# Softmax attention on one core: the maxima's negation one reduction later, sums normalised a pair at a time, maxima sixteen ahead in place of twenty

## The chip, the cores and the metric

The kernel runs on one core of one Trainium2 chip. The metric is device time in microseconds of one execution; the median of three executions of the kernel before is 1983.7 us (1981.62 to 1983.73).

## The reference, cut to what matters

Two blocks run one after the other; the change lies in the second block's attention (16 heads of 8 features each). Every query of every head takes a softmax over 2048 keys:

```
q = _apply_rope(_rms_norm(x @ wq.T), cos, sin) / sqrt(8)
k = _apply_rope(_rms_norm(x @ wk.T), cos, sin)
scores = einsum('bqhd,bkhd->bhqk', q, k)
attn = softmax(scores, axis=-1)
out = einsum('bhqk,bkhd->bqhd', attn, v) @ wo.T
```

Two sequences of 2048 tokens with 16 heads give 32 square score matrices of 2048 x 2048, which the kernel computes twice: once to find each query's maximum, once, transposed and with the maximum subtracted, for the exponential.

## The kernel before, in words

`softmax_attention` (from line 1322) works on pairs of heads: 16 pairs (8 of each sequence), each cut into 4 chunks of 512 queries, 64 chunks in all. In what follows n is a chunk whose exponentials are under way, m one whose maxima are.

**Maxima.** A chunk has 32 units. For unit a TensorE multiplies 128 queries with 512 keys (`maximum`, line 1489) into one of four banks (3 to 6), and VectorE reduces the bank to one column (line 1631). TensorE's unit u waits until the reduction of unit u - 4 is done (line 1486). Behind the 32nd reduction VectorE waits for all of them (line 1635) and takes the largest over the key blocks, negated (`at_neg`, line 1636). GpSimd turns that into three bfloat16 parts (`parts`, lines 1421 to 1431: five small operations, each waiting for the one ahead). TensorE transposes the parts (`shifts`, line 1499), and ScalarE copies them in two operations into spare rows of the queries (`take_shifts`, line 1582). So every score comes out with the maximum already subtracted.

**Scores.** A chunk has 32 steps s. TensorE makes 128 keys x 512 queries (`score`, line 1509) into one of three banks (0 to 2), ScalarE takes the exponential (line 1590), and every second step TensorE multiplies with the values (`weigh`, line 1525, eight matmuls at a time). A bank is used again when the turn three turns back has been read (`free_bank`). The transposed parts and the transposed sums take turns in the same three banks.

**Sums.** ScalarE copies the chunk's result out of bank 7 (`take_sums`, line 1596) after exponential 3 of the next chunk, TensorE transposes it (line 1536) after step 11, ScalarE copies that to rows (`read_sums`, line 1602). VectorE takes the reciprocal of the 8 sums (`invert`, line 1624), and GpSimd multiplies the 64 columns with them (`normalise_sums`, line 1439). VectorE's `invert(m - 2)` stands right behind the negation of chunk m.

**Order on TensorE.** It is written out by hand. A prologue issues all 32 maxima of chunk 0 and the first AHEAD = 20 of chunk 1, `shifts(0)` behind the maximum 10 and scores 0 to 3 beside the last four. The main loop then issues one score and one maximum at each step: beside score s of chunk n stands maximum s - 4 + AHEAD counted from chunk n + 1's first. With AHEAD = 20 the last maximum of chunk n + 1 (number 31) stands at s = 15, the first one of chunk n + 2 (number 0) at s = 16. `shifts(n + 1)` stands behind step 27, where with AHEAD = 20 the maximum number 11 of chunk n + 2 stands.

GpSimd's order in chunk n is: `parts(n + 1)`, `normalise_sums(n - 1)`, at the first chunk of a pair two copies of the next pair's values (line 1411), and in the last two pairs four gathers of rows for the stage behind (line 1762). SyncE loads the queries and keys of coming pairs. The stage behind (`finish`, line 1642) begins when every engine has ended this one.

Of the kernel before, what the change touches and what calls it, by code (L numbers as in the profile page):

```python
# [7 lines left out]
ALU = mybir.AluOpType  # L8
ACT = mybir.ActivationFunctionType
X_AXIS = mybir.AxisListType.X  # L10

P = 128
# [5 lines left out]
TPC = CHUNK // P  # L18
HEADS = 16
DK = D // HEADS  # L20
# [32 lines left out]
def bc(ap, shape):  # L53
    return ap.to_broadcast(shape)
# [1267 lines left out]
def softmax_attention(k, U, V, attn, gather):  # L1322

    nc = k.nc
    bank = k.bank
    NK = SEQ // P
    QC = SEQ // CHUNK  # L1330
    NPAIRS = BATCH * PAIRS
    NCHUNKS = NPAIRS * QC
# [4 lines left out]
    UNITS = 2 * TPC * PER_TILE  # L1337
# [3 lines left out]
    S_BANK, M_BANK, O_BANK = 0, 3, 7  # L1341
    PR = 16
    G = 4
    AHEAD = 20
    FIRST_SCORES = G


# [1 line left out]
    NSUMS = 2 * TPC * (DK + 1)  # L1349
    GATHERED = TILES // (2 * QC)  # L1350
    with ExitStack() as ctx:
        sem = stage_semaphores(k, ctx, "at_")
        sb = lambda name, shape, dt=F32: ctx.enter_context(nc.sbuf_tensor(f"at_{name}", shape, dt))
        queries, keys, values = k.queries, k.keys, k.values
        probs = k.shared[:, :].rearrange("p (n t) -> p n t", n=PR)
        tops = sb("tops", [P, 2, 2 * TPC, PER_TILE])
        neg = sb("neg", [P, 2 * TPC])
        left = sb("left", [P, 2, 2 * TPC])
        shift = sb("shift", [P, TPC, P], BF16)
        sumsT = sb("sumsT", [P, 2, HALF])  # L1360
        inv = sb("inv", [P, 2, 2 * TPC])
        sums_rows = sb("sums_rows", [P, 2, NSUMS])
        (cleared, copy_allowed, v_loaded, m_ready, m_out, neg_ready, shift_step, shift_ready, shiftT_ready, shift_in, s_ready,
         p_ready, p_used, sums_out, turned, sums_read, inv_ready, attn_out) = (
            sem(n) for n in ("cleared", "copy_allowed", "v_loaded", "m_ready", "m_out", "neg_ready", "shift_step", "shift_ready",
# [34 lines left out]
        @block.gpsimd  # L1400
        def _(pool):
            pool.memset(shift[:, :, :], 0.0).then_inc(cleared, 1)  # L1402

            def before_copy():
                pool.sem_inc(copy_allowed, 1)

            def load(pair):
                before_copy()
                for h in range(2):
                    at = pair * 2 * DK + h * DK  # L1410
                    nc.gpsimd.tensor_copy(values[pair % 2][:, :, h, 0:DK], V[:, :, at:at + DK]).then_inc(v_loaded, 1)

            def parts(m):
                pool.wait_ge(neg_ready, m + 1)
                if m:
                    pool.wait_ge(shiftT_ready, m)
                of = lambda i: shift[:, :, :].rearrange("p t (h r) -> p h t r", h=2)[:, :, :, SHIFT + i]
                src = neg[:, :].rearrange("p (h t) -> p h t", h=2)
                rest = [left[:, i, :].rearrange("p (h t) -> p h t", h=2) for i in range(2)]
                before_copy()  # L1420
                nc.gpsimd.tensor_copy(of(0), src).then_inc(shift_step, 1)  # L1421
                pool.wait_ge(shift_step, 4 * m + 1)
                nc.gpsimd.tensor_tensor(rest[0], src, of(0), ALU.subtract).then_inc(shift_step, 1)
                pool.wait_ge(shift_step, 4 * m + 2)
                before_copy()
                nc.gpsimd.tensor_copy(of(1), rest[0]).then_inc(shift_step, 1)
                pool.wait_ge(shift_step, 4 * m + 3)
                nc.gpsimd.tensor_tensor(rest[1], rest[0], of(1), ALU.subtract).then_inc(shift_step, 1)
                pool.wait_ge(shift_step, 4 * m + 4)
                before_copy()  # L1430
                nc.gpsimd.tensor_copy(of(2), rest[1]).then_inc(shift_ready, 1)

            def normalise_sums(n):
                pair, c = divmod(n, QC)
                pool.wait_ge(sums_read, n + 1)
                pool.wait_ge(inv_ready, n + 1)
                of = sums_rows[:, n % 2, :].rearrange("p (t h e) -> p t h e", h=2, e=DK + 1)
                to = attn[:, c * TPC:(c + 1) * TPC, pair * 2 * DK:(pair + 1) * 2 * DK]
                nc.gpsimd.tensor_tensor(to.rearrange("p t (h e) -> p t h e", h=2), of[:, :, :, 0:DK],
                                        bc(inv[:, n % 2, :].rearrange("p (t h) -> p t h", h=2).unsqueeze(3), [P, TPC, 2, DK]), ALU.mult).then_inc(attn_out, 1)  # L1440

            pool.wait_ge(cleared, 1)
            load(0)
            parts(0)
            for n in range(NCHUNKS):
                pair, c = divmod(n, QC)
                if n + 1 < NCHUNKS:
                    parts(n + 1)
                if n:
                    normalise_sums(n - 1)  # L1450
                if c == 0 and pair + 1 < NPAIRS:

                    if pair:
                        pool.wait_ge(p_used, n * S // G)
                    load(pair + 1)
                if pair >= NPAIRS - 2:
                    first = (n - (NPAIRS - 2) * QC) * GATHERED
                    for t in range(first, first + GATHERED):
                        gather(pool, t)
            normalise_sums(n)  # L1460

        @block.tensor
        def _(pe):
# [111 lines left out]
        @block.scalar  # L1575
        def _(act):
            def take_shifts(m):
                act.wait_ge(shiftT_ready, m + 1)
                pair, c = divmod(m, QC)
                for h in range(2):  # L1580
                    rows = slice(h * HEAD_ROWS + SHIFT, h * HEAD_ROWS + SHIFT + PARTS)
                    nc.scalar.activation(queries[pair % 2][rows, c * CHUNK:(c + 1) * CHUNK],  # L1582
                                         bank[rows, bank_of("shifts", m), 0:HALF].bitcast(BF16), ACT.Copy).then_inc(shift_in, 1)

            def exponential(n, s):
                act.wait_ge(s_ready, n * S + s + 1)
                groups = n * (S // G) + s // G + 1 - PR // G
                if s % G == 0 and groups > 0:
                    act.wait_ge(p_used, groups)
                nc.scalar.activation(probs[:, s % PR, :], bank[:, bank_of("score", n, s), :], ACT.Exp).then_inc(p_ready, 1)  # L1590

            def take_sums(n):
                act.wait_ge(p_used, (n + 1) * (S // G))
                if n >= 2:
                    act.wait_ge(turned, n - 1)
                nc.scalar.activation(sumsT[:, n % 2, :], bank[:, O_BANK, 0:HALF], ACT.Copy).then_inc(sums_out, 1)

            def read_sums(n):
                act.wait_ge(turned, n + 1)
                if n >= 2:  # L1600
                    act.wait_ge(attn_out, n - 1)
                nc.scalar.activation(sums_rows[:, n % 2, :], bank[:, bank_of("sums", n), 0:NSUMS], ACT.Copy).then_inc(sums_read, 1)

            take_shifts(0)
            for n in range(NCHUNKS):
                for s in range(S):
                    exponential(n, s)
                    if s == COPY_AT - 1 and n:
                        take_sums(n - 1)
                    if s == SUMS_AT - 1 and n:  # L1610
                        read_sums(n - 1)
                    if s == SHIFTS_AT - 1 and n + 1 < NCHUNKS:
                        take_shifts(n + 1)
            take_sums(n)
            read_sums(n)

        @block.vector
        def _(dve):
            def invert(n):
                dve.wait_ge(sums_read, n + 1)  # L1620
                if n >= 2:
                    dve.wait_ge(attn_out, n - 1)
                of = sums_rows[:, n % 2, :].rearrange("p (t h e) -> p t h e", h=2, e=DK + 1)
                nc.vector.reciprocal(inv[:, n % 2, :].rearrange("p (t h) -> p t h", h=2), of[:, :, :, DK]).then_inc(inv_ready, 1)

            for m in range(NCHUNKS):
                for u in range(UNITS):
                    h, qt, kb = maximum_of(u * WIDE)
                    at = unit_bank(m * UNITS + u)
                    dve.wait_ge(m_ready, m * UNITS + u + 1)  # L1630
                    nc.vector.tensor_reduce(tops[:, m % 2, h * TPC + qt, kb // WIDE:kb // WIDE + 1],  # L1631
                                            bank[:, at:at + WIDE, :].rearrange("p b n -> p (b n)"), X_AXIS, ALU.max).then_inc(m_out, 1)
                if m:
                    dve.wait_ge(shift_ready, m)
                dve.wait_ge(m_out, (m + 1) * UNITS)
                nc.vector.tensor_reduce(neg[:, :], tops[:, m % 2], X_AXIS, ALU.max, negate=True).then_inc(neg_ready, 1)  # L1636
                if m >= 2:
                    invert(m - 2)
            for n in range(NCHUNKS - 2, NCHUNKS):
                invert(n)  # L1640

def finish(k, w, attn, g_rows, r, out_dram):

# [259 lines left out]
```

## Time and profile before

| | us |
|---|---|
| median of 3 executions | 1983.7 |
| the profiled execution | 1984.38 |
| its span, first to last instruction | 1982.3 |
| from the first reduction of the attention to its last product | 664.16 to 1958.13 |
| VectorE busy in the whole span | 1591.2 (80%) |
| TensorE busy in the whole span | 1718.6 (87%) |
| ScalarE busy in the whole span | 1440.3 (73%) |

The profiled execution took 2.1 us more than its span and lies 0.7 us above the median. Starts are microseconds from the span's start. In a timeline a row is one instruction, or several of one line merged (x32), with the start of the first and the time from there to the end of the last; idle time ahead of it stands in brackets with what ended it. Instructions of one engine overlap: the next one begins before the result of the one ahead is written, so the distance of two starts is shorter than a duration.

### The profile page before, as it was taken

To read this page: it belongs to the slowest core of one execution; us is meant where nothing else is said; L and a number is where in the kernel's file an instruction comes from. 1 tells how busy PE (TensorE), PEld (TensorE's weight loads), DVE (VectorE), ACT (ScalarE), POOL (GpSimd) and SP (SyncE) were. 2 spreads that over 40 slices of the span, in tenths; PEclk is the share of its full clock that TensorE was granted. 3 is DMA by queue.
4 is the path that set the end of the run, shared out by engine and by line. 5 is a ranking of instruction groups with operands and counts; after the bars stand their busy time and mean duration, and the time that the engine had idled before them with its cause. 6 is when DMAs were issued, how large, how long until landed. Compare 5 with 4: busy or idle time off the path is not lost. (4 is left out here: it accounts for less than half of the span.)

```text
span 1982.3 us, 41860 instructions
## 1 busy us (share of the span) xinstructions
PE 1718.6 (87%) x16109; PEld 717.3 (36%) x16109; DVE 1591.2 (80%) x2845; ACT 1440.3 (73%) x2873; POOL 318.5 (16%) x668
## 2 busy tenths in 40 slices
PE   4883879465669999999999999999999999999997
PEld 4453653253359422222222222222222222222224
DVE  3751435755373799999999999999999999999982
ACT  2111547423335289999999999999999999999997
POOL 2272007525030000000000000000000000002221
PEclk9896998657669699999999999999999999999998
DMA  8014111313003001010010110100101101001001
GB/s 257 17 53 113 49 49 53 92 34 86 0 2 68 18 1 18 2 18 9 11 18 1 18 18 2 18 10 10 18 3 17 18 2 18 13 6 25 16 13 52
DMA packets 64294, 61.83 MB, mean 31 GB/s; under 512 B 10752, under 2 KB 52736, under 8 KB 64096
## 3 DMA queue, kind: packets, MB, share of 16 engines
q1 hardware_dynamic: 57952, 46.56, 10.5%
q0 software_dynamic: 6144, 12.60, 2.1%
q8 instruction: 128, 2.10, 0.5%
q14 instruction: 70, 0.57, 0.1%
HBM read 23.21 MB, written 22.94 MB: 23 GB/s over the span
## 5 line engine op out<-in xcount | busy, mean ns | idle before, releaser
L1631 DVE TENSOR_REDUCE at_tops<-bank 128x1 f32<-128x512 f32 x2048 | 1234.1, 683 | 16.3 <-PE bank L1489 10.5
L1590 ACT ACTIVATE experts_then_probs<-bank 128x512 f32<-128x512 f32 x2048 | 1093.4, 600 | 75.6 <-PE bank L1509 54.9
L1509 PE MATMUL bank<-queries,keys 64*128 64x512 bf16 x2048 | 631.4, 383 | 45.3 <-ACT experts_then_probs L1590 38.4
L1489 PE MATMUL bank<-keys,queries 64*128 64x512 bf16 x2048 | 656.7, 389 | 4.9 <-POOL at_shift L1402 4.3
L1525 PE MATMUL bank<-experts_then_probs,values 128*32 128x256 f32 x8192 | 642.1, 391 | 0.0
L1509 PEld LDWEIGHTS bank<-queries,keys 64*128 64x128 bf16 x2048 | 128.4, 93 | 503.5 <-ACT experts_then_probs L1590 412.0
L1525 PEld LDWEIGHTS bank<-experts_then_probs,values 128*32 128x32 f32 x8192 | 167.9, 108 | 311.3 <-ACT experts_then_probs L1590 207.5
L1421 POOL CAST at_shift<-at_neg 128x8 bf16<-128x8 f32 x64 | 13.9, 217 | 1112.9 <-DVE at_neg L1636 1112.9
L1489 PEld LDWEIGHTS bank<-keys,queries 64*128 64x128 bf16 x2048 | 148.5, 93 | 65.7 <-DVE at_tops L1631 50.3
L653 DVE COPY ep_weights<-WB 128x642 f32 x72 | 35.8, 497 | 88.9 <-DVE ep_slots L664 46.6
L1582 ACT ACTIVATE queries<-bank 3x512 bf16<-3x512 bf16 x128 | 75.4, 589 | 32.8 <-PE bank L1499 29.5
L680 ACT ACTIVATE ep_hT<-bank,ep_weights 128x128 f32<-128x128 f32 x144 | 45.1, 365 | 48.8 <-PE bank L622 48.7
L287 POOL DMA_INDIRECT sorted_pairs<-g_rows,pair_slot x64 | 62.4, 975 | 51.3 <-DVE pair_slot L534 32.1
L1007 ACT ACTIVATE ro_rest<-bank 128x512 f32<-128x512 f32 x16 | 9.5, 596 | 81.6 <-PE bank L959 81.6
L622 PE MATMUL bank<-ep_slotsT,ep_weights 128*128 128x128 f32 x288 | 51.8, 304 | 19.3 <-DVE ep_weights L653 19.3
L975 PE MATMUL bank<-identb,ro_parts 128*128 128x128 bf16 x192 | 23.5, 294 | 51.8 <-ACT query_parts L999 38.8
L958 PE MATMUL bank<-ro_wqk,xnT 128*128 128x512 f32 x64 | 56.2, 976 | 6.9 <-DVE ro_qk L1142 4.3
L1133 DVE TENSOR_REDUCE ro_st<-ro_rest 128x64 f32<-128x512 f32 x16 | 11.0, 685 | 61.8 <-ACT ro_rest L1007 61.8
L1287 DVE COPY ffn_w<-experts_then_probs 128x512 f32 x39 | 23.2, 594 | 40.6 <-PE bank L1253 37.6
L814 DVE RECIPROCAL qg_den<-qg_den 128x512 f32<-128x512 f32 x8 | 26.8, 3353 | 34.4 <-ACT qg_den L783 34.4
L717 POOL DMA_INDIRECT g_rows<-made_of_pairs,pair_slot x32 | 31.0, 969 | 141.8 <-SPq L698 132.4
L622 PEld LDWEIGHTS bank<-ep_slotsT,ep_weights 128*128 128x128 f32 x288 | 38.4, 194 | 31.3 <-DVE ep_weights L653 29.7
(252 smaller groups left out, 1597.1 us busy)
## 6 DMA issues: line engine op xcount, KB each, us to landing
queries<-query_parts SPq DMA_DIRECT2D x192, 32.0 KB
keys<-key_parts SPq DMA_DIRECT2D x192, 32.0 KB
sorted_pairs<-zeros SPq DMA_DIRECT2D x16, 288.0 KB, 3.3
ep_slots<-sorted_pairs SPq DMA_DIRECT2D x6, 768.0 KB, 9.2
made_of_pairs<-ep_slots SPq DMA_DIRECT2D x6, 768.0 KB, 4.1
sorted_tokens<-zeros SPq DMA_DIRECT2D x8, 312.0 KB, 3.4
x<-in_L_attn_x_dram SPq DMA_DIRECT2D x4, 512.0 KB, 6.0
experts_then_probs<-in_L_ffn_W_dram SPq DMA_DIRECT2D x1, 2048.0 KB, 10.0
```

The source lines that it names most:

```text
L287: pool.indirect_dma_start(sorted_dram, bass.IndirectOffsetOnAxis(ap=r0.slot[i][:, t:t + 1], axis=0), rows[:, t, :], None).then_inc(scatter ...
L622: mm = nc.tensor.matmul(bank[:, H_BANK + u, i * P:(i + 1) * P], wt[:, u, i * P:(i + 1) * P], slotsT[:, j // TPC % TR, j % TPC * P:(j % TPC ...
L653: nc.vector.tensor_copy(wt[:, j % R, :], WB[:, bass.ds(at, STRIDE0)]).then_inc(w_ready, 1)
L680: nc.scalar.activation(hT[:, u, i * P:(i + 1) * P], bank[:, H_BANK + u, i * P:(i + 1) * P], ACT.Relu, bias=wt[:, u, B1_AT + i:B1_AT + i + ...
L717: pool.indirect_dma_start(y[i][:, t, :], None, made_dram, bass.IndirectOffsetOnAxis(ap=r0.slot[i][:, t:t + 1], axis=0)).then_inc(gathered[ ...
L958: nc.tensor.matmul(bank[:, first_bank(g) + t, :], xnT[:, at:at + P], wqk[:, :], start=True, stop=True)
L1489: mm = nc.tensor.matmul(bank[:, unit_bank(u) + a % WIDE, :], queries[pair % 2][rows, at:at + P], keys[pair % 2][rows, kb * CHUNK:(kb + 1) ...
L1509: nc.tensor.matmul(bank[:, bank_of("score", n, s), :], keys[pair % 2][rows, at:at + P], queries[pair % 2][rows, c * CHUNK:(c + 1) * CHUNK] ...
L1525: mm = nc.tensor.matmul(bank[32 * j:32 * j + 32, O_BANK, 0:HALF], values[pair % 2][:, kt, h, :], probs[:, s % PR, q * HALF:(q + 1) * HALF] ...
L1582: nc.scalar.activation(queries[pair % 2][rows, c * CHUNK:(c + 1) * CHUNK], bank[rows, bank_of("shifts", m), 0:HALF].bitcast(BF16), ACT.Cop ...
L1590: nc.scalar.activation(probs[:, s % PR, :], bank[:, bank_of("score", n, s), :], ACT.Exp).then_inc(p_ready, 1)
L1631: nc.vector.tensor_reduce(tops[:, m % 2, h * TPC + qt, kb // WIDE:kb // WIDE + 1], bank[:, at:at + WIDE, :].rearrange("p b n -> p (b n)"), ...
```

## The change

Four edits go together. AHEAD becomes 16. The negation of chunk m is issued behind the first reduction of chunk m + 1 instead of ahead of it (for the last chunk, at the end). The rows of sums of the four chunks of a pair are kept in one buffer of two halves, one for each pair. VectorE takes one reciprocal of 32 columns for a pair (behind the second reduction of chunk 4p + 3, for pair p - 1), and GpSimd makes one product of 256 columns for it, behind `parts` in the second chunk of the next pair.

```
-    AHEAD = 20
+    AHEAD = 16
...
-        inv = sb("inv", [P, 2, 2 * TPC])
-        sums_rows = sb("sums_rows", [P, 2, NSUMS])
+        inv = sb("inv", [P, 2, QC * 2 * TPC])
+        sums_rows = sb("sums_rows", [P, 2, QC * NSUMS])
...
-            def normalise_sums(n):
-                pair, c = divmod(n, QC)
-                pool.wait_ge(sums_read, n + 1)
-                pool.wait_ge(inv_ready, n + 1)
...
+            def normalise_sums(pair):
+                pool.wait_ge(sums_read, QC * (pair + 1))
+                pool.wait_ge(inv_ready, pair + 1)
...
-                if n:
-                    normalise_sums(n - 1)
+                if c == 1 and pair:
+                    normalise_sums(pair - 1)
...
-            normalise_sums(n)
+            normalise_sums(pair)
...
-                if n >= 2:
-                    act.wait_ge(attn_out, n - 1)
-                nc.scalar.activation(sums_rows[:, n % 2, :], ...
+                pair, c = divmod(n, QC)
+                if c == 0 and pair >= 2:
+                    act.wait_ge(attn_out, pair - 1)
+                nc.scalar.activation(sums_rows[:, pair % 2, c * NSUMS:(c + 1) * NSUMS], ...
...
+            def invert(pair):
+                dve.wait_ge(sums_read, QC * (pair + 1))
+                if pair >= 2:
+                    dve.wait_ge(attn_out, pair - 1)
...
+            def negate(m):
+                if m:
+                    dve.wait_ge(shift_ready, m)
+                dve.wait_ge(m_out, (m + 1) * UNITS)
+                nc.vector.tensor_reduce(neg[:, :], tops[:, m % 2], X_AXIS, ALU.max, negate=True).then_inc(neg_ready, 1)
...
-                if m:
-                    dve.wait_ge(shift_ready, m)
-                dve.wait_ge(m_out, (m + 1) * UNITS)
-                nc.vector.tensor_reduce(neg[:, :], tops[:, m % 2], X_AXIS, ALU.max, negate=True).then_inc(neg_ready, 1)
-                if m >= 2:
-                    invert(m - 2)
-            for n in range(NCHUNKS - 2, NCHUNKS):
-                invert(n)
+                    if u == 0 and m:
+                        negate(m - 1)
+                    if u == 1 and m >= 3 + QC and (m - 3) % QC == 0:
+                        invert((m - 3) // QC - 1)
+            negate(m)
+            for pair in range(NPAIRS - 1, NPAIRS):
+                invert(pair)
```

## Rows read from the trace of the kernel before

**Rows 1.** Windows: start:end and length, busy us (instructions), clock, DMA share, GB/s
```profile
663.50:691.44 27.94, 27.36 (x53) 4.92 (x54) 27.24 (x47) 2.37 (x3) 1.58 (x7) 0.50 0.00 1
691.44:699.96 8.52, 8.52 (x45) 2.06 (x44) 7.78 (x13) 5.63 (x11) 0.00 (x0) 0.50 0.00 0
704.26:1927.40 1223.14, 1178.69 (x12406) 358.77 (x12398) 1209.40 (x2107) 1148.79 (x2233) 109.92 (x425) 1.00 0.08 12
```

**Rows 2.** Timeline of VectorE: start, us, engine, line, operation
```profile
664.16 19.23 DVE L1631 TENSOR_REDUCE at_tops<-bank 128x1 f32<-128x512 f32 x32 [8.57 <-PE bank L1489]
683.42 0.19 DVE L1636 TENSOR_REDUCE at_neg<-at_tops 128x8 f32<-128x32 f32 x1
683.53 0.68 DVE L1631 TENSOR_REDUCE at_tops<-bank 128x1 f32<-128x512 f32 x1
...
1216.66 0.19 DVE L1636 TENSOR_REDUCE at_neg<-at_tops 128x8 f32<-128x32 f32 x1
1216.76 0.20 DVE L1624 RECIPROCAL at_inv<-at_sums_rows 128x8 f32<-128x8 f32 x1
1216.88 19.36 DVE L1631 TENSOR_REDUCE at_tops<-bank 128x1 f32<-128x512 f32 x32
...
1236.35 0.19 DVE L1636 TENSOR_REDUCE at_neg<-at_tops 128x8 f32<-128x32 f32 x1
```

**Rows 3.** Who waited for L1631 from 721 to 1927: us, times
```profile
  PEld bank L1489: 24.5, 122
```

**Rows 4.** Timeline of one chunk, TensorE: score 12, 22, 24, 26, shifts, next score 12; then VectorE's unit
```profile
1213.61 0.39 PE L1509 MATMUL bank<-queries,keys 64*128 64x512 bf16 x1
...
1219.14 0.39 PE L1509 MATMUL bank<-queries,keys 64*128 64x512 bf16 x1
...
1220.27 0.39 PE L1509 MATMUL bank<-queries,keys 64*128 64x512 bf16 x1
...
1221.46 0.39 PE L1509 MATMUL bank<-queries,keys 64*128 64x512 bf16 x1
...
1222.09 0.40 PE L1499 MATMUL bank<-identb,at_shift 128*128 128x128 bf16 x4
...
1233.30 0.39 PE L1509 MATMUL bank<-queries,keys 64*128 64x512 bf16 x1
...
1233.76 0.69 DVE L1631 TENSOR_REDUCE at_tops<-bank 128x1 f32<-128x512 f32 x1
```

**Rows 5.** Timeline around the shifts and behind: ScalarE's copies, TensorE's score 7
```profile
1223.00 1.20 ACT L1582 ACTIVATE queries<-bank 3x512 bf16<-3x512 bf16 x2
...
1209.50 0.39 PE L1509 MATMUL bank<-queries,keys 64*128 64x512 bf16 x1 [0.38 <-ACT experts_then_probs L1590]
```

**Rows 6.** Timeline of chunk 62: score 12, scores 26 and 27, shifts, ScalarE's copies
```profile
1924.36 0.39 PE L1509 MATMUL bank<-queries,keys 64*128 64x512 bf16 x1
...
1932.09 0.60 PE L1509 MATMUL bank<-queries,keys 64*128 64x512 bf16 x2
1932.63 0.38 PE L1499 MATMUL bank<-identb,at_shift 128*128 128x128 bf16 x4
...
1933.62 1.21 ACT L1582 ACTIVATE queries<-bank 3x512 bf16<-3x512 bf16 x2
```

**Rows 7.** Timeline of GpSimd: the last of the five part operations
```profile
1218.38 0.22 POOL L1431 CAST at_shift<-at_left 128x8 bf16<-128x8 f32 x1 [0.17 <-POOL at_left L1428]
```

**Rows 8.** Timeline of the prologue: TensorE's first shifts, then ScalarE
```profile
688.39 0.61 PE L1499 MATMUL bank<-identb,at_shift 128*128 128x128 bf16 x4
...
689.03 1.20 ACT L1582 ACTIVATE queries<-bank 3x512 bf16<-3x512 bf16 x2 [29.50 <-PE bank L1499]
690.25 1.28 ACT L1590 ACT_TABLE_LOAD   x1
692.12 4.46 ACT L1590 ACTIVATE experts_then_probs<-bank 128x512 f32<-128x512 f32 x8 [0.58 <-PE bank L1509]
```

**Rows 9.** The last product in the timeline; groups by form of two longer relatives
```profile
1957.84 0.29 POOL L1439 TENSOR_TENSOR xnT<-at_sums_rows,at_inv 128x64 f32<-128x64 f32 x1 [8.20 <-DVE at_inv L1624]
...
L1140 DVE RECIPROCAL ro_st<-ro_st 128x64 f32<-128x64 f32 x16 | 8.8, 553 | 0.6 <-ACT ro_st L1016 0.6
...
L192 POOL TENSOR_TENSOR g_rows<-ln_centred,ln_stats 128x1024 f32<-128x1024 f32 x8 | 15.2, 1895 | 37.1 <-DVE ln_stats L178 37.1
```

More of the change, by code:

```diff
@@ L1431, in parts @@
                 nc.gpsimd.tensor_copy(of(2), rest[1]).then_inc(shift_ready, 1)
-            def normalise_sums(n):
-                pair, c = divmod(n, QC)
-                pool.wait_ge(sums_read, n + 1)
-                pool.wait_ge(inv_ready, n + 1)
-                of = sums_rows[:, n % 2, :].rearrange("p (t h e) -> p t h e", h=2, e=DK + 1)
-                to = attn[:, c * TPC:(c + 1) * TPC, pair * 2 * DK:(pair + 1) * 2 * DK]
+            def normalise_sums(pair):
+                pool.wait_ge(sums_read, QC * (pair + 1))
+                pool.wait_ge(inv_ready, pair + 1)
+                of = sums_rows[:, pair % 2, :].rearrange("p (t h e) -> p t h e", h=2, e=DK + 1)
+                to = attn[:, :, pair * 2 * DK:(pair + 1) * 2 * DK]
                 nc.gpsimd.tensor_tensor(to.rearrange("p t (h e) -> p t h e", h=2), of[:, :, :, 0:DK],
-                                        bc(inv[:, n % 2, :].rearrange("p (t h) -> p t h", h=2).unsqueeze(3), [P, TPC, 2, DK]), ALU.mult).then_inc(attn_out, 1)
+                                        bc(inv[:, pair % 2, :].rearrange("p (t h) -> p t h", h=2).unsqueeze(3), [P, NK, 2, DK]),
+                                        ALU.mult).then_inc(attn_out, 1)
             pool.wait_ge(cleared, 1)
@@ L1599, in read_sums @@
                 act.wait_ge(turned, n + 1)
-                if n >= 2:
-                    act.wait_ge(attn_out, n - 1)
-                nc.scalar.activation(sums_rows[:, n % 2, :], bank[:, bank_of("sums", n), 0:NSUMS], ACT.Copy).then_inc(sums_read, 1)
+                pair, c = divmod(n, QC)
+                if c == 0 and pair >= 2:
+                    act.wait_ge(attn_out, pair - 1)
+                nc.scalar.activation(sums_rows[:, pair % 2, c * NSUMS:(c + 1) * NSUMS], bank[:, bank_of("sums", n), 0:NSUMS], ACT.Copy).then_inc(sums_read, 1)
             take_shifts(0)
@@ L1618, in _ @@
         def _(dve):
[L1619 to L1624, printed above, removed]
+            def invert(pair):
+                dve.wait_ge(sums_read, QC * (pair + 1))
+                if pair >= 2:
+                    dve.wait_ge(attn_out, pair - 1)
+                of = sums_rows[:, pair % 2, :].rearrange("p (t h e) -> p t h e", h=2, e=DK + 1)
+                nc.vector.reciprocal(inv[:, pair % 2, :].rearrange("p (t h) -> p t h", h=2), of[:, :, :, DK]).then_inc(inv_ready, 1)
+            def negate(m):
[3 more added lines that the diff above has]
+                nc.vector.tensor_reduce(neg[:, :], tops[:, m % 2], X_AXIS, ALU.max, negate=True).then_inc(neg_ready, 1)
             for m in range(NCHUNKS):
```

## The prediction, written before the changed kernel ran

> **What bounds the kernel now.** I read the windows first, then the timeline of each engine over one chunk, since two engines are nearly full. Between 704 and 1927 us VectorE is busy 1209.4 of 1223.1 us and TensorE 1178.7, at a granted clock of 1.00 (2.4 GHz) [rows 1]. A chunk takes 1236.35 - 1216.66 = 19.69 us from negation to negation [rows 2], and the 62 chunks between 704.26 and 1927.40 average 19.73 [rows 1]; I take 19.70. By busy time this is VectorE's stage, but the chunk's timeline shows a loop through both engines. A reduction is issued every 0.598 us ((19.23 - 0.68) / 31 in the first chunk [rows 2]), so 32 need 19.14; 0.56 is over.
> - 0.39 of it is negation and reciprocal. With a plain reduction between them, the last one and the next chunk's first would start 0.60 apart. The last of 32 starts 0.68 before the row's end, at 1235.56; the negation starts 0.79 later, since it waits until that one is written, and the reciprocal and the next reduction follow at 0.10 and 0.12 [rows 2]. That is 1.01, and the reduction behind gives 0.04 back.
> - 0.18 is VectorE waiting for TensorE at score step 12: TensorE issues at 1233.30, and the reduction starts at 1233.76, 0.46 later [rows 4], 0.18 behind its 0.598 place.
>
> TensorE in turn waits for a bank from VectorE 122 times in 61 chunks, twice in each [rows 3]. Free of VectorE, two steps take 1.106 us (five such pairs from 1213.61 to 1219.14); steps 22 to 24 take 1.13, 24 to 26 take 1.19 [rows 4]. So **VectorE costs TensorE 0.024 + 0.084 = 0.108 us a chunk ahead of score 26.** Another 0.08 behind step 26 (shifts 0.63 behind score 26, against 0.54 in chunk 62 [rows 4, 6]) costs nothing: ScalarE is the later one there, with its copies 1.54 behind score 26 [rows 4, 5], and 1.53 in chunk 62, where the shifts come sooner [rows 6]. The rest of the loop, from there to the next step 12, is TensorE and ScalarE alone; score 7, say, waits 0.38 for an exponential [rows 5]. So without any wait for VectorE a chunk takes 19.70 - 0.108 = **19.59 us**. Chunk 62, whose second half has no maxima, goes through steps 12 to 26 in 7.73 us [rows 6] against 7.85 in a usual chunk [rows 4], the same 0.11.
>
> **The change, part by part.**
> 1. *Negation behind a reduction.* Its wait is for reductions that ended before, so the drain of 0.19 (0.79 less 0.60) should go; what is left is its own place of about 0.10 (683.42 to 683.53, where no reciprocal follows [rows 2]). The unknown is whether a small operation behind a running reduction starts at 0.60; the nearest rows bound it by 0.60 and 0.79, and I take 0.60, as for reductions in a row.
> 2. *One reciprocal for four.* Three of four chunks lose 0.12. The fourth holds one of 32 columns: 8 columns take 0.20 [rows 2], 64 take 0.553 [rows 9], so 0.0063 a column and 0.35 for 32, or 0.12 + 0.15 = 0.27 of VectorE's time. Mean 0.07 instead of 0.12.
> 3. *VectorE's leg,* in us from the issue of score 12 (t = 0; beside it now unit 24). Unit 24 starts at 0.46, unit 31 at 4.65, unit 0 at 5.24, the negation at 5.84, unit 1 at 5.94, units 2 and 3 at 6.54 and 7.14; each is written 0.68 later, and TensorE follows some 0.06 behind. TensorE, undisturbed, comes to steps 25, 26 and 27 at 6.86, 7.74 and 7.97 (seven pairs of 1.106, and 0.22 to the odd step) and needs units 1, 2 and 3, ready at 6.68, 7.28 and 7.88. All three are met, by 0.18, 0.46 and 0.09. The 32-column reciprocal moves units 2 and 3 by 0.27: step 27 then waits 0.18, but its score is issued ahead of it and ScalarE's copies stand 1.54 behind score 26, so it stays hidden as the 0.08 does today. VectorE needs 19.14 + 0.10 + 0.07 = 19.31, less than 19.59.
> 4. *The shift chain,* which AHEAD = 16 puts closer to its user. From the start of the negation to the end of the last part operation it takes 18.60 - 16.66 = 1.94 [rows 2, 7]. New: 5.84 + 1.94 = 7.78, about 0.1 more to reach TensorE; the shifts come at 7.74 + 0.54 = 8.28. It is met with 0.4 to spare, where today it has 3.5 (1222.09 less 1218.60 [rows 4, 7]). Nothing stands between on GpSimd: its parts are ahead of its product, value copies and gathers in each chunk, and those end long before the next negation, 19 us on.
> 5. *GpSimd's product* of 256 columns: 0.29 for 64 and 1.895 for 1024 [rows 9] give 0.0017 a column, so 0.61. It waits for the reciprocal under one reduction longer than today; nothing in the loop waits for it. Cost 0, except at the end. ScalarE's changed wait is met four chunks earlier.
> 6. *SyncE's loads* wait for uses of the probabilities, which come with the scores; they move with them.
>
> **The sum.** Chunks 0 to 61 hold the wait: 62 x 0.108 = 6.7 us gained. The prologue gains too: two maxima fewer stand ahead of the first shifts (2 x 0.598), and 0.12 of drain goes (0.22 gained, 0.10 for the negation). So the shifts come at 687.07, the copies end at 688.91, and the exponential's table, 1.28 us, is loaded at 690.2. Score 0, four maxima earlier, is ready before that; the first exponential starts near 690.3 instead of 692.12 [rows 8], 1.8 us. What follows runs at the 1.2 GHz level (granted 0.50) until 699.96, behind 28 us of one maximum at a time [rows 1]. If the clock rises at the same instant, the 1.8 us won are worth half, 0.9; if TensorE's denser work, now earlier, lifts it earlier, up to 2.8. I take 1.8, the shift alone. The end loses the longer reciprocal (0.15) and product (0.32), which stand alone behind the last sums: -0.5. Sum: 6.7 + 1.8 - 0.5 = **8.0 us**. The profiled execution would give 1984.4 - 8.0 = 1976.4; it is 0.7 above the median, so the median is forecast at 1983.7 - 8.0 = **1975.7 us**.
>
> **A rule that speaks against it.** The rows show 0.79 between reduction and negation with the wait, and 0.598 between reductions without [rows 2]. The Trainium skill (VectorE: DVE Perf Modes, "The DRAIN you can't avoid") says that a semaphore between two VectorE instructions costs nothing extra, as the pipeline empties either way, and that their number is what to cut. By that rule moving the negation gains nothing and only the reciprocals count.
>
> **Rivals.**
> - *The drain stays* (that rule's outcome as a mechanism here): the negation at 0.79. Then units 1, 2 and 3 are ready at 6.87, 7.47 and 8.07; step 25 waits 0.01 and step 27 0.10, hidden. Gain 62 x 0.10 + 1.6 - 0.5 = 7.3, so 1976.4. For it: negation and reciprocal start at a wait today. Against: reductions overlap by 0.08. 8%.
> - *VectorE still throttles.* If the negation disturbs the stream more than 0.18 beyond my 0.10 (a small read from another memory between two bank reads is not shown without a wait), steps 25 to 27 wait as they do now, and only the prologue is won: 1983.7 - 1.8 + 0.5 = 1982.4, no change. Against: negation and reciprocal side by side cost 0.22. 15%.
> - *The shifts come late,* slower. Place: TensorE's wait ahead of the transposes. The chain is 1.94 and may be 2.4; ScalarE hides about 0.16 more, and the 0.108 is given back first. For the whole to be slower by 0.2% (4 us; 0.2% is about what a measurement of this kernel can tell from no change) the chain must pass 2.4 + 0.16 + 0.108 + 5.3 / 62, some 2.75 us. At 3.0 the chunk is 19.59 + 0.44 = 20.03: 62 x 0.33 - 1.3 = 19 us, 2003. For: the slack falls from 3.5 to 0.4. Against: nothing is put ahead of the five operations on GpSimd, and what they wait for, each other, is as before. 6%.
> - *The whole of VectorE's gain comes through:* period 19.31, 62 x 0.39 + 1.3 = 25 us, 1958. It would need TensorE and ScalarE to have slack that chunk 62 doesn't show. 3%.
> - The forecast: 68%.
>
> **Range and chances.** Own range of the forecast: prologue 0.9 to 2.8, period gain 0.108 +- 0.03 (1.9 us), execution noise 1 us: 1972 to 1979.5. Reaching toward the no-change case on one side and a little of the large gain on the other: 1971.5 to 1981.5. Faster: 68 + 8 + 3, and a little of the forecast's low tail off: 0.78. Same: 0.16. Slower: 0.06.
>
> **What would show it.** Right: chunk period 19.59; one wait of TensorE for VectorE at most, at step 27 of each fourth chunk; VectorE's busy share down and its idle time in waits for TensorE up, about 0.3 us a chunk at steps 8 to 12; negation 0.60 behind its reduction; parts ended 0.4 before the shifts; first exponential near 690.3. Wrong: a period of 19.70 with the bank waits still twice a chunk (VectorE), or an idle TensorE ahead of the shifts ended by GpSimd (late chain), or a period below 19.5.

## The result, and the profile after

The changed kernel takes 1973.2 us (median of 5, 1971.8 to 1973.5) against 1983.7: a ratio of 0.9948 with an interval of 0.9936 to 0.996, so 10.5 us less. The forecast was 1975.7 us, 8.0 less, and its range holds the result. The profiled execution has a span of 1971.5 us.

VectorE's timeline after; a row is a start, a length, the engine, line, operation and count, and in brackets what ended the idle time:

```profile
1214.74 0.17 DVE L1632 TENSOR_REDUCE at_neg<-at_tops 128x8 f32<-128x32 f32 x1
1214.84 13.83 DVE L1639 TENSOR_REDUCE at_tops<-bank 128x1 f32<-128x512 f32 x23
1228.94 5.47 DVE L1639 TENSOR_REDUCE at_tops<-bank 128x1 f32<-128x512 f32 x9 [0.27 <-PE bank L1490]
1234.33 0.17 DVE L1632 TENSOR_REDUCE at_neg<-at_tops 128x8 f32<-128x32 f32 x1
1234.42 13.83 DVE L1639 TENSOR_REDUCE at_tops<-bank 128x1 f32<-128x512 f32 x23
...
1274.19 0.34 DVE L1626 RECIPROCAL at_inv<-at_sums_rows 128x32 f32<-128x32 f32 x1
1274.45 15.73 DVE L1639 TENSOR_REDUCE at_tops<-bank 128x1 f32<-128x512 f32 x26
```

They answer to [rows 2]. From negation to negation it is 19.59 us, the forecast number. The negation starts 0.60 behind its reduction (5.47 long for nine, the last one starts at 1233.73) and the next reduction 0.09 behind it. VectorE now waits 0.27 us for TensorE in one place, unit 24 at 1228.94, beside score 12. The reciprocal of 32 columns takes 0.34 and holds VectorE for 0.26; the forecast was 0.35 and 0.27.

TensorE's timeline, answering to [rows 4]: scores 12, 22, 24 and 26, the shifts, and score 12 of the next chunk:

```profile
1228.48 0.39 PE L1510 MATMUL bank<-queries,keys 64*128 64x512 bf16 x1
...
1234.01 0.39 PE L1510 MATMUL bank<-queries,keys 64*128 64x512 bf16 x1
...
1235.12 0.39 PE L1510 MATMUL bank<-queries,keys 64*128 64x512 bf16 x1
...
1236.23 0.39 PE L1510 MATMUL bank<-queries,keys 64*128 64x512 bf16 x1
...
1236.77 0.39 PE L1500 MATMUL bank<-identb,at_shift 128*128 128x128 bf16 x4
...
1248.07 0.39 PE L1510 MATMUL bank<-queries,keys 64*128 64x512 bf16 x1
```

Steps 22 to 24 and 24 to 26 take 1.11 us each, where they took 1.13 and 1.19. Who waited for whom between the two engines (us, times, from 721 to 1920), first what VectorE waited for, then what waited for VectorE, answering to [rows 3]:

```profile
  PE bank L1490: 12.6, 46
...
  PEld bank L1490: 3.2, 15
```

122 waits of TensorE have become 15, one in each fourth chunk: the one at step 27 that the large reciprocal causes. On the other side stand 46 waits of VectorE for TensorE, 0.27 us in each of the three chunks of four that have no reciprocal; the kernel before has 3, 0.7 us in all.

GpSimd's timeline after, its last part operation and its product, answering to [rows 7, 9]:

```profile
1236.04 0.22 POOL L1432 CAST at_shift<-at_left 128x8 bf16<-128x8 f32 x1 [0.17 <-POOL at_left L1429]
...
1275.36 0.63 POOL L1439 TENSOR_TENSOR xnT<-at_sums_rows,at_inv 128x256 f32<-128x256 f32 x1
```

ScalarE's timeline in the prologue, answering to [rows 8]:

```profile
689.18 1.20 ACT L1583 ACTIVATE queries<-bank 3x512 bf16<-3x512 bf16 x2 [28.16 <-PE bank L1500]
690.40 1.28 ACT L1591 ACT_TABLE_LOAD   x1
691.69 4.03 ACT L1591 ACTIVATE experts_then_probs<-bank 128x512 f32<-128x512 f32 x8
```

The parts end at 1236.26, 0.51 before the shifts at 1236.77. The product takes 0.63 us (forecast 0.61). The first reduction starts at 665.64 in this execution, so the first exponential comes 26.05 us behind it, against 27.96 before: 1.9 us sooner (forecast 1.8), and right behind its table, as forecast.

Where the span's 10.8 us went, stretch by stretch, from both traces:

| stretch | before | after | gain |
|---|---|---|---|
| to the first reduction (stages that the change leaves alone) | 664.16 | 665.64 | -1.5 |
| from there to the copies of chunk 1 | 46.35 | 43.28 | 3.1 |
| from there to the last read of sums | 1246.71 | 1237.96 | 8.8 |
| from there to the end | 25.05 | 24.62 | 0.4 |

The first line is a difference between the two executions, in stages that are the same in both kernels. Of the third line 6.8 us are 0.11 in each of 61 chunks. The other 2.0 are two single chunks of the execution before, 0.35 and 1.64 us longer than their neighbours; the changed kernel's profiled execution has none. Such long chunks came and went between the kernels tried below. Several had none; the one with AHEAD alone had 0.35 twice, in the same two chunks as the kernel before. What makes them is not shown.

### The profile page after: what moved, and what is told of

It is laid out like the page before. It is cut to its first block and busy times, and to the rows that moved or that the text cites. A ratio compares the mean times of both kernels' runs of the same rounds, so it can differ in the third digit from the quotient of the medians.

```text
span 1971.5 us, 41620 instructions
## 1 busy us (share of the span) xinstructions
PE 1708.5 (87%) x16109; PEld 705.7 (36%) x16109; DVE 1581.8 (80%) x2797; ACT 1439.5 (73%) x2873; POOL 312.9 (16%) x620
## 3 DMA queue, kind: packets, MB, share of 16 engines
q1 hardware_dynamic: 57952, 46.56, 10.5%
## 5 line engine op out<-in xcount | busy, mean ns | idle before, releaser
L1490 PE MATMUL bank<-keys,queries 64*128 64x512 bf16 x2048 | 644.2, 388 | 4.7 <-POOL at_shift L1403 4.3
L1490 PEld LDWEIGHTS bank<-keys,queries 64*128 64x128 bf16 x2048 | 137.7, 93 | 30.6 <-DVE at_tops L1639 25.1
```

What stands on the lines that cost most here:

```text
L1490: mm = nc.tensor.matmul(bank[:, unit_bank(u) + a % WIDE, :], queries[pair % 2][rows, at:at + P], keys[pair % 2][rows, kb * CHUNK:(kb + 1) ...
```

## The experiments

The time of a chunk is the distance of two reads of sums by ScalarE, from each kernel's own timeline; a few single chunks are longer, as above. Each time is the median of a kernel's executions, each ratio is to the kernel before, with its interval in brackets. Times of the kernel before beside the runs were 1983.5 to 1984.8 us.

**1. Each part by itself.** AHEAD alone:

```diff
-    AHEAD = 20
+    AHEAD = 16
```

> The kernel before with AHEAD = 16 alone; negation and reciprocals stay where they were. Theory (a loop of TensorE and ScalarE of 19.59 us a chunk, delayed where VectorE's reductions come late): with the pause of 0.39 us now between units 31 and 0 beside steps 19 and 20, unit 1 is written 6.96 us behind score 12, and step 25 wants it at 6.86; so 0.10 of the 0.108 us a chunk stays lost, the period stays 19.69, and only the prologue gains, some 3 us: 1980.7 us. Rival (the shift chain is what the twenty ahead are for): the period rises. Rival (AHEAD is where the period's gain came from): 19.59 us a chunk, 1974 us.

Measured: 1978.7 us, ratio 0.9971 (0.9959 to 0.9983); 19.69 to 19.70 us a chunk, 122 waits of TensorE for VectorE. So AHEAD does not shorten the period. From the first reduction to the copies of chunk 1 it takes 42.55 us against 46.35, a gain of 3.8 where some 3 were expected (point 4 in the next section splits it).

The negation alone, in the kernel before:

```diff
-                if m:
-                    dve.wait_ge(shift_ready, m)
...
-                if m >= 2:
-                    invert(m - 2)
+                    if u == 0 and m:
+                        negate(m - 1)
+                        if m >= 3:
+                            invert(m - 3)
+            negate(m)
+            invert(m - 2)
```

> The kernel before with the negation (and the reciprocal of 8 columns right behind it) moved behind the next chunk's first reduction; AHEAD = 20, reciprocals and products for each chunk. Theory of the loop: the drain of 0.19 us goes, which is more than the 0.108 that VectorE cost TensorE, so the period is 19.59 us and the whole 1983.7 - 6.7 - 0.1 = 1976.9 us. Rival (VectorE simply bounds the stage): the period falls by the whole 0.19 to 19.51 us, 1972 us. Rival (a semaphore wait costs nothing, only the count of instructions does): 19.70 us, 1983.7 us.

Measured: 1976.7 us, 0.9956 (0.9942 to 0.997). ScalarE's timeline, two reads of sums:

```profile
1211.26 0.24 ACT L1602 ACTIVATE at_sums_rows<-bank 128x72 f32<-128x72 f32 x1
1230.85 0.24 ACT L1602 ACTIVATE at_sums_rows<-bank 128x72 f32<-128x72 f32 x1
```

VectorE's timeline in the same kernel:

```profile
1212.00 3.08 DVE L1637 TENSOR_REDUCE at_tops<-bank 128x1 f32<-128x512 f32 x5 [0.20 <-PE bank L1489]
1215.00 0.17 DVE L1630 TENSOR_REDUCE at_neg<-at_tops 128x8 f32<-128x32 f32 x1
1215.09 0.19 DVE L1624 RECIPROCAL at_inv<-at_sums_rows 128x8 f32<-128x8 f32 x1
1215.20 16.18 DVE L1637 TENSOR_REDUCE at_tops<-bank 128x1 f32<-128x512 f32 x27
```

19.59 us a chunk by the reads of sums: this one edit is enough for the whole gain of the period. It is not 19.51, so VectorE's time alone doesn't set it; and it is not 19.70. TensorE waits for VectorE nowhere between 721 and 1920 us, and VectorE waits for TensorE once a chunk (61 times, 12.2 us in all).

The pair's sums alone (the changed kernel with AHEAD = 20 and `negate(m)` behind the loop over the units again):

> The changed kernel with AHEAD = 20 and the negation ahead of the next chunk as before, so only one reciprocal of 32 columns and one product of 256 for four chunks. Theory of the loop: three chunks of four lose the 0.12 us of the small reciprocal, more than the 0.108, and take 19.59 us; the fourth carries 0.27 in place of 0.12 and takes 19.85 us. Mean 19.65: 1983.7 - 2.8 + 0.5 = 1981.4 us. Rival (the large reciprocal or the large product disturbs the reductions more than its own length): the fourth chunk is above 20 us and the whole is 1984 us or more.

Measured: 1980.5 us, 0.998 (0.9971 to 0.9989). ScalarE's timeline, three reads of sums:

```profile
1251.86 0.24 ACT L1604 ACTIVATE at_sums_rows<-bank 128x72 f32<-128x72 f32 x1
1271.47 0.24 ACT L1604 ACTIVATE at_sums_rows<-bank 128x72 f32<-128x72 f32 x1
1291.28 0.24 ACT L1604 ACTIVATE at_sums_rows<-bank 128x72 f32<-128x72 f32 x1
```

The rows show one chunk of each kind; of four chunks three take 19.61 and one 19.81, where 19.59 and 19.85 were expected. Taking the small reciprocal away gave 0.09 us of its 0.12, and the large one, which holds VectorE for 0.26, makes its chunk 0.20 longer than the others. So this edit too, without the other, gains most of the 0.11, but only in three chunks of four.

AHEAD = 20 in the changed kernel:

> The changed kernel with AHEAD = 20 again. Theory: AHEAD is worth the prologue alone, 1.9 us of earlier first exponential and 1.1 us of earlier clock rise; the period is 19.59 us, and 19.68 in each fourth chunk, where the large reciprocal holds unit 5 back by 0.09 us: 1973.2 + 2.8 + 1.4 = 1977.4 us. Rival (AHEAD = 16 also gave the period's gain): 19.70 us a chunk, 1983 us.

Measured: 1976.3 us, 0.9958 (0.9945 to 0.9972); 19.59, and 19.61 in each fourth chunk. By the medians AHEAD = 16 is worth 3.1 us in the changed kernel. In the two profiled executions 1.3 us of this lie between the first reduction and the copies of chunk 1, and 0.5 in the chunks; the other 1.2 lie in the stages ahead and behind, which AHEAD leaves alone, and that AHEAD makes them is not shown. The pair's sums are worth next to nothing once the negation is moved (1976.3 with them, 1976.7 without).

**2. Is it the drain?** The wait of the negation is made to cover the reduction that has just been issued:

```diff
-                dve.wait_ge(m_out, (m + 1) * UNITS)
+                dve.wait_ge(m_out, min((m + 1) * UNITS + 1, NCHUNKS * UNITS))
```

> The changed kernel with the negation waiting also for the reduction ahead of it, which it does not need, so that it starts only when that one is written. Theory: the negation starts 0.79 us behind the reduction in place of 0.60, VectorE has 0.28 us a chunk to spare, and unit 1 is just in time: period 19.59 to 19.60 us, 1973 to 1974 us. Rival (the drain was what the change gained): 19.70 us a chunk, 1980 us. Rival (a wait costs VectorE nothing): the negation starts at 0.60 still.

Measured: 1974.8 us, 0.9957 (0.9943 to 0.9971); 19.61 to 19.63 us a chunk. VectorE's timeline with this wait:

```profile
1212.79 1.28 DVE L1639 TENSOR_REDUCE at_tops<-bank 128x1 f32<-128x512 f32 x2
1214.18 0.19 DVE L1632 TENSOR_REDUCE at_neg<-at_tops 128x8 f32<-128x32 f32 x1
1214.28 1.88 DVE L1639 TENSOR_REDUCE at_tops<-bank 128x1 f32<-128x512 f32 x3
```

The second reduction starts at 1213.39 (1.28 less 0.68), the negation 0.79 behind it: the drain of 0.19 is back by one number in a wait. It costs 0.03 us a chunk. So the wait does cost VectorE 0.19, and the changed kernel, with its small reciprocals gone, has the room to hide nearly all of it, as the rival "the drain stays" had it. TensorE waits for VectorE once a chunk again (62 times, 15.5 us from 721 to 1920), and yet the chunk is 0.03 longer, not 0.25: a sum of waits is not what they cost. The same two instructions start 0.60 apart when the wait is for older reductions and 0.79 when it is for the one just ahead. The Trainium skill (VectorE: DVE Perf Modes, "The DRAIN you can't avoid") has the semaphore cost nothing extra; these starts disagree.

Experiments 1 and 2 together: the drain taken out is enough for the period, and so, within 0.02 us, is the small reciprocal taken out with the drain left in, in every chunk that doesn't hold the large one. The two gains overlap and must not be added.

**3. Is VectorE the bound at all now?** Each reduction reads half of its columns, which leaves out half of the keys, so the result is another softmax; the factor in the exponential keeps it finite.

```diff
-                nc.scalar.activation(probs[:, s % PR, :], bank[:, bank_of("score", n, s), :], ACT.Exp).then_inc(p_ready, 1)
+                nc.scalar.activation(probs[:, s % PR, :], bank[:, bank_of("score", n, s), :], ACT.Exp, scale=0.0625).then_inc(p_ready, 1)
...
-                                            bank[:, at:at + WIDE, :].rearrange("p b n -> p (b n)"), X_AXIS, ALU.max).then_inc(m_out, 1)
+                                            bank[:, at:at + WIDE, 0:CHUNK // 2].rearrange("p b n -> p (b n)"), X_AXIS, ALU.max).then_inc(m_out, 1)
```

> The changed kernel with each of the 2048 reductions over 256 of its 512 columns, and the exponential taken of a sixteenth of the score so that it stays finite: the maxima are those of half the keys and the softmax is another one; all instructions and waits stay. Theory: VectorE's reductions are issued every 0.33 us in place of 0.60, and the chunk still takes 19.59 us, since the loop runs through TensorE and ScalarE alone; the prologue of 48 maxima is set by TensorE at its lower clock (0.45 us each) and ends some 7 us sooner: 1966 us. Rival (VectorE bounds the chunk): the period falls far below 19.5 us.

Measured: 1964.3 us, 0.9906 (0.9889 to 0.9922). VectorE's waits from 721 to 1900 us (engine, waited for, total, times, longest):

```profile
DVE at_tops L1639 <- PE bank L1490: 426.6, 946, 0.9
```

Two reads of sums in ScalarE's timeline there:

```profile
1216.49 0.24 ACT L1604 ACTIVATE at_sums_rows<-bank 128x72 f32<-128x72 f32 x1
1236.08 0.24 ACT L1604 ACTIVATE at_sums_rows<-bank 128x72 f32<-128x72 f32 x1
```

VectorE idles a third of the time, and a chunk takes 19.59 us as in the changed kernel. The 9 us (7 were expected) came in the prologue, where the first exponential stands 16.46 us behind the first reduction in place of 26.05. So 19.59 us is what TensorE and ScalarE take by themselves.

**4. The shift chain, the slower rival.** Two runs with fewer maxima ahead:

> The changed kernel with AHEAD = 15: the parts reach TensorE about 8.5 us behind score 12, the shifts have their place at 8.28, so 0.1 to 0.2 us late and all of it hidden: period 19.59 us, prologue 0.5 us shorter, 1972.7 us. Rival (late parts cost what they are late): 19.7 to 19.8 us a chunk, 1980 us or more.

> The changed kernel with AHEAD = 14: the negation stands 1.2 us later against the shifts. The parts would reach TensorE some 9.1 us behind score 12 and the shifts have their place at 8.28: late by 0.7 to 0.8 us. As the prediction had it, ScalarE hides 0.16 of that: 62 chunks of 19.59 + 0.6, some 2010 us. A second reading of the rows lets the lateness be hidden up to some 0.5 us, since the copies stand 1.54 behind score 26 and TensorE waits for an exponential at score 31 anyway: 19.59 + 0.25, some 1988 us. Rival (the chain is not near its user at all): 1973 us.

Measured: AHEAD = 15 2111.4 us, 1.0645 (1.0628 to 1.0662), 21.78 us a chunk; AHEAD = 14 2329.9 us, 1.1746 (1.1727 to 1.1765), 25.00. None of the expectations held. TensorE waits nowhere for GpSimd; what differs is when the matmuls start. TensorE's timeline with AHEAD = 14:

```profile
1201.46 0.39 PE L1510 MATMUL bank<-queries,keys 64*128 64x512 bf16 x1
1201.69 0.38 PE L1490 MATMUL bank<-keys,queries 64*128 64x512 bf16 x1
1201.90 0.38 PE L1510 MATMUL bank<-queries,keys 64*128 64x512 bf16 x1
1202.12 0.38 PE L1490 MATMUL bank<-keys,queries 64*128 64x512 bf16 x1
```

A score and its maximum start 0.22 apart, where the kernel before and the changed one start them 0.01 apart. The two use 64 of the 128 rows each, one head's; the maximum takes the head that the score of its step doesn't, but only if AHEAD is a multiple of four. With 14 all 32 pairs of a chunk are on the same rows, with 15 half of them. The heads swapped:

```diff
-    AHEAD = 16
+    AHEAD = 14
...
-        maximum_of = lambda a: (1 - head_of(a), ...
+        maximum_of = lambda a: (head_of(a), ...
```

> AHEAD = 14 as in the run that took 2330 us, but each maximum takes the other head, so that the score and the maximum of one step are again of different heads and use different halves of TensorE's rows. Theory: the 357 us came from pairs on the same rows, which run one behind the other; with the heads swapped they start 0.01 us apart again, and what is left of AHEAD = 14 is the late shift chain: 0.75 us late, 0.55 of it hidden, 0.5 us gained in the prologue: a period of 19.6 to 19.8 us, 1973 to 1985 us. Rival (the 357 us came from late shifts): above 2300 us again.

Measured: 1985.7 us, 1.001 (1.0001 to 1.002), 19.77 us a chunk; 344 us of the 357 are gone. Score and maximum start 0.01 us apart or less again, against 0.22. The Trainium skill (TensorE: Matmul & The Clock Gate, "Packing small matmuls — row/col tiling") says that matmuls on different row groups run side by side in the array; the pairs agree.

With the pairs mended, AHEAD = 14 shows the late chain that I had meant to show, and so does a longer chain at AHEAD = 16:

```diff
+                for i in range(4):
+                    nc.gpsimd.tensor_tensor(rest[1], src, src, ALU.subtract).then_inc(shift_step, 1)
+                    pool.wait_ge(shift_step, 8 * m + i + 1)
                 before_copy()
                 nc.gpsimd.tensor_copy(of(0), src).then_inc(shift_step, 1)
-                pool.wait_ge(shift_step, 4 * m + 1)
+                pool.wait_ge(shift_step, 8 * m + 5)
...
```

> The changed kernel with four more small subtractions, each waiting for the one ahead, between the negation and the first part on GpSimd: the chain of 1.94 us becomes some 3.3, and the parts come 1.0 us behind the place of the shifts. By the prediction 0.16 us of that is hidden: 19.59 + 0.84, 2025 us. By the second reading of the rows up to 0.5 is hidden: 19.59 + 0.5, 2004 us. Rival (the chain is nowhere near its user): 1973 us.

Measured: 1979.2 us, 0.9973 (0.9961 to 0.9984), 19.66 us a chunk. TensorE's timeline there, score 27 and the shifts:

```profile
1219.27 0.38 PE L1513 MATMUL bank<-queries,keys 64*128 64x512 bf16 x1
1219.27 0.38 PE L1493 MATMUL bank<-keys,queries 64*128 64x512 bf16 x1
1220.20 0.40 PE L1503 MATMUL bank<-identb,at_shift 128*128 128x128 bf16 x4 [0.56 <-POOL at_shift L1435]
```

The same of the kernel with AHEAD = 14 and swapped heads, with ScalarE's copies:

```profile
1200.50 0.38 PE L1510 MATMUL bank<-queries,keys 64*128 64x512 bf16 x1
1200.50 0.38 PE L1490 MATMUL bank<-keys,queries 64*128 64x512 bf16 x1
1201.56 0.40 PE L1500 MATMUL bank<-identb,at_shift 128*128 128x128 bf16 x4 [0.68 <-POOL at_shift L1432]
1201.99 1.20 ACT L1583 ACTIVATE queries<-bank 3x512 bf16<-3x512 bf16 x2 [0.21 <-PE bank L1500]
```

And ScalarE's copies in the changed kernel, which follow the shifts of 1236.77 above:

```profile
1237.76 1.20 ACT L1583 ACTIVATE queries<-bank 3x512 bf16<-3x512 bf16 x2
```

Undisturbed, the shifts start 0.32 behind score 27 (1236.77 in the changed kernel, its score 27 at 1236.45). Here they start 0.93 and 1.06 behind: 0.61 and 0.74 late. The chunks are 0.07 and 0.18 longer. So **some 0.55 us of lateness is hidden**, the same in both. ScalarE's copies show where: in the changed kernel they start 0.99 behind the shifts, since ScalarE is busy until then, and in the two late kernels 0.43 behind. Ahead of the copies ScalarE idles 0.02 us in the changed kernel, 0.10 in the one with the longer chain and 0.21 in the one with AHEAD = 14 and swapped heads, and the two differences, 0.08 and 0.19, are what the chunks got longer. The four operations made the chain 3.0 us long, not the expected 3.3; with 0.16 hidden, as the prediction had it, the chunk would still have been some 20.0 us (19.59 and 0.61 less 0.16), and it was 19.66.

**5. What bounds the changed kernel.** First the banks:

```diff
-    R = 3
-    MR = 4 // WIDE
-    S_BANK, M_BANK, O_BANK = 0, 3, 7
+    R = 4
+    MR = 3 // WIDE
+    S_BANK, M_BANK, O_BANK = 0, 4, 7
```

> The changed kernel with four banks for scores and three for maxima, in place of three and four. Theory: what bounds the chunk now is the loop of TensorE and ScalarE, whose waits (score 7 for an exponential, scores 30 and 31 for copies and exponential, 1.1 us a chunk together) come from three banks; with four they mostly go, and VectorE becomes the bound at 19.31 us: 1973.2 - 62 x 0.28, some 1956 us. Rival (TensorE needs its lead of four units to feed VectorE over its own holes of 1.3 us): VectorE starves, and the chunk takes 19.6 us or more, 1973 us or above.

Measured: 1988.2 us, 1.0022 (1.0012 to 1.0033), 19.78 us in most chunks and 19.98 in each fourth. Waits from 721 to 1920 us (who waits, for what, total, times, longest):

```profile
PEld bank L1490 <- DVE at_tops L1639: 126.0, 427, 0.5
```

The rival holds: TensorE, three units ahead at most, waits for VectorE seven times a chunk, and VectorE still waits for TensorE once, 0.30 us at step 12. The fourth bank is worth more to the maxima.

Then the order of the weighing matmuls, against the wait at score 7 [rows 5]. The first eight of a chunk move from behind score 7 to behind score 6:

```diff
-                    if s % G == 1 and g:
+                    if s % G == (1 if g else 2):
                         weigh(n, g, 0)
                     if s % G == 3:
-                        if g == 0:
-                            weigh(n, g, 0)
                         weigh(n, g, 1)
```

> The changed kernel with the first eight weighing matmuls of a chunk behind score 6 in place of behind score 7. Theory: TensorE now stands 0.38 us at score 7 until exponential 4 is done and then weighs for 1.0 us; with eight of the sixteen put into that wait, score 8 comes 0.35 us sooner, the loop of TensorE and ScalarE falls to some 19.25 us, below VectorE's 19.31, and VectorE becomes the bound: 1973.2 - 62 x 0.28, some 1956 us. Rival (the copy of the sums, which the first weighing waits for, ends too late for the gap): no more than 0.1 us a chunk, 1967 us or more. Rival (VectorE bounds already): 1973 us.

Measured: **1955.1 us, 0.9857 (0.9841 to 0.9874)**, 29 us less than the kernel before and 18 less than the changed one, 19.28 us a chunk. TensorE's timeline from score 6 to score 8 in the changed kernel:

```profile
1223.61 0.39 PE L1510 MATMUL bank<-queries,keys 64*128 64x512 bf16 x1
...
1224.38 0.39 PE L1510 MATMUL bank<-queries,keys 64*128 64x512 bf16 x1 [0.38 <-ACT experts_then_probs L1591]
...
1224.70 1.07 PE L1526 MATMUL bank<-experts_then_probs,values 128*32 128x256 f32 x16
1225.70 0.39 PE L1510 MATMUL bank<-queries,keys 64*128 64x512 bf16 x1
```

And in the one with the moved weighing:

```profile
1215.65 0.39 PE L1510 MATMUL bank<-queries,keys 64*128 64x512 bf16 x1
...
1215.97 0.64 PE L1526 MATMUL bank<-experts_then_probs,values 128*32 128x256 f32 x8
1216.55 0.39 PE L1510 MATMUL bank<-queries,keys 64*128 64x512 bf16 x1
...
1216.86 0.64 PE L1526 MATMUL bank<-experts_then_probs,values 128*32 128x256 f32 x8
1217.44 0.39 PE L1510 MATMUL bank<-queries,keys 64*128 64x512 bf16 x1
```

From score 6 to score 8 it takes 1.79 us in place of 2.09, and the chunk is 0.31 shorter. Between 721 and 1900 us VectorE waits for TensorE nowhere, and TensorE waits for VectorE 26 times, 5.0 us in all: now VectorE bounds the chunk, near the 19.31 that the prediction gave for it. The loop of TensorE and ScalarE by itself would take some 19.29 (an estimate, 19.59 less the 0.30), so the two are about level.

## Why the prediction was right, point by point

1. *The bound.* Right: a loop of TensorE and ScalarE of 19.59 us, which VectorE delayed by 0.108. The trace after shows 19.59, and half-width reductions, with VectorE idle a third of the time, leave it there. Busy shares alone (VectorE's 99% of the stage) would have put the gain at 0.39 a chunk, the 3% rival. One sign was wrong: VectorE's busy share did not go down. It is 1199.88 of 1213.74 us from 704.26 to 1918, 98.9% as before [rows 1]; its waits for TensorE took the place of the drain. And one figure was added wrongly: 1.01 less 0.60 less the 0.04 given back is 0.37, not 0.39. Nothing was worked out from it.
2. *The negation.* Right: the drain of 0.19 went (0.60 in place of 0.79), its own place is 0.09 (forecast 0.10), and moved by itself it gives the whole period. It is not the only way to it: with the drain back in the changed kernel 0.08 of the 0.11 stay.
3. *The reciprocal and the product.* Right to 0.02 us each (0.34 and 0.63 measured, 0.35 and 0.61 forecast), and right that step 27 of each fourth chunk waits and that this costs nothing.
4. *The prologue.* The earlier first exponential was right (1.9 us sooner, right behind its table), but the term was sized too small: 1.8 in the sum with bounds of 0.9 and 2.8, and 3.1 measured, above both. Part of the 3.1 is TensorE's clock. Its windows in the changed kernel (start:end and length; busy us and instructions of TensorE's matmuls, its weight loads, VectorE, ScalarE and GpSimd; granted clock, DMA share, GB/s):

```profile
665.60:690.00 24.40, 23.96 (x48) 4.38 (x44) 24.36 (x42) 0.80 (x2) 1.10 (x6) 0.50 0.01 1
690.00:697.90 7.90, 7.90 (x37) 1.94 (x36) 7.16 (x13) 5.97 (x11) 0.00 (x0) 0.50 0.00 0
697.90:710.00 12.10, 12.10 (x134) 3.37 (x132) 12.05 (x22) 11.63 (x22) 1.50 (x7) 0.99 0.01 2
```

   The 2.4 GHz level comes some 32.4 us behind the first reduction, against 35.8 before [rows 1, 2]. I had given an earlier rise the upper bound, 2.8 us, and chosen the middle. The other kernels' traces let the two be told apart (us behind the first reduction):

   | kernel | AHEAD | level rises at | copies of chunk 1 at |
   |---|---|---|---|
   | before; pair's sums alone | 20 | 35.8 | 46.35, 46.34 |
   | negation alone; changed, AHEAD = 20 | 20 | 32.4 | 44.61, 44.60 |
   | changed; weighing moved | 16 | 32.4 | 43.28, 43.36 |
   | AHEAD alone; drain put back | 16 | 29.0 | 42.55, 42.55 |

   With the rise at the same instant, AHEAD = 16 is worth 1.3 us (44.60 less 43.28), more than the half of 1.8 that I had allowed it. A rise 3.4 us sooner goes with 1.75 us at AHEAD = 20, the drain gone included, and with 0.7 at 16. So of the 3.1 us in the profiled executions 1.3 are AHEAD's, and the rest is nearly all the clock's. The same AHEAD and the same drain, there or gone, go with the same rise, which speaks for the kernel setting it; how it would is not shown, and neither is that the few executions with a profile didn't fall so by chance.
5. *The end.* The longer reciprocal and product cost 0.5 us as forecast, 0.35 + 0.63 against 0.20 + 0.29. Even so the stretch to the end is 0.4 us shorter in the profiled execution. In the stage behind, its clock is at the lower level for 6.8 us, against 10.2 before; that this is the whole reason is not shown. In the kernels with the pair's sums alone and with the drain put back, where it is 10.2 as well, the stretch is 25.55 us, the forecast 0.5 longer than before.
6. *The shift chain.* Right that it is met with time to spare: 0.4 forecast, 0.51 measured. Wrong in a term that the result didn't need: of a late chain I let ScalarE hide 0.16 us, and 0.55 are hidden. The slower rival's threshold was so 0.4 us further off than written. What truly lay beside AHEAD = 16, pairs on the same rows for any number that is not a multiple of four, was no rival of mine.
7. *The sum.* 6.7 of 8.0 us were the chunks, in 62 of them; measured 6.8, in 61. With the prologue at 3.1 and the end at -0.5 it comes to 9.4 of the 10.5 measured between the medians. Of the 1.1 left, the long single chunks of the kernel before may be a part; that was not shown. The prologue's 1.3 us above its term were covered by the range only since the chunks came in at their forecast.

## What to carry to other kernels

When two engines are both nearly full, don't take either's busy time for the bound: lay one period of both side by side, find where each waits for the other, and add up only the delays that a third engine's schedule doesn't absorb. An instruction that waits for the one just issued on its own engine can be worth moving behind the next one: here the wait held VectorE for 0.19 us, of which the chunk had felt 0.11. After it is moved, the next gain, nearly three times as large a chunk, lay in work put into a wait of TensorE, in the loop that had become the bound. When an order is shifted against another one, check which units the two were paired on.

## What was not expected of the hardware

Two matmuls of 64 rows and 512 columns start 0.01 us apart on different halves of TensorE's rows and 0.22 apart on the same ones. With all 32 pairs of a chunk on the same rows the chunk took 25.00 us, and 19.77 with the heads swapped, 5.2 less. A wait for the instruction just ahead on VectorE held the next one for 0.19 us; a wait for an older one left the starts 0.60 apart, as between reductions. Transposes that started 0.74 us late on TensorE made the chunk 0.18 longer, since ScalarE's copies behind them had 0.55 in hand.
